# Router head of feed-forward 1 inside the causal attention, and output pieces ahead of query stores

## The reference

```python
x = x + _L0_attn_a_ref(_layernorm(x), Wqkv, Wo)   # 32 heads of 16, one k and v, ALiBi, causal
x = x + _L0_ffn_ref(_layernorm(x), c1_w, c2_w, w1, w2t)
x = x + _L0_attn_b_ref(_layernorm(x), wq, wk, wv, wo)  # 32 heads of 128 on 8, rope, window 128
x = x + _L0_ffn_ref(_layernorm(x), c1_w, c2_w, w1, w2t)
```

```python
inter = xf @ c1_w.T @ c2_w.T
idx = argmax(inter.reshape(n, 56, 32), -1) + arange(0, 1792, 32)
h = relu(einsum('bkm,bm->bk', w1[idx], xf)); out = einsum('bk,bkm->bm', h, w2t[idx])
```

## Time and profile before

| | us |
|---|---|
| median of 3 runs | 2777.52 |
| lowest, highest | 2772.59, 2779.67 |
| profiled execution | 2770.34 |
| its span, first to last instruction | 2768.6 |
| barrier between attention and feed-forward 1, from the span's start | 543.6 to 544.8 |
| PE busy in the span | 2594.3 (94%) |
| DVE, ACT, POOL busy | 1721.9, 1309.1, 1054.8 |
| mean granted clock of PE | 0.964 of 2.4 GHz |

### The profile page before, as it was taken

The page is one execution under the profiler, slowest core; times in us unless marked ns, Lnnn a source line. Parts: engine busy times, 40 slices in busy tenths (PEclk is TensorE's granted clock), DMA queues, the critical chain, the costliest instruction groups (busy, mean ns, idle before and its releaser), DMA issues. The chain is left out here.

```text
span 2768.6 us, 41665 instructions
## 1 busy us (share of the span) xinstructions
PE 2594.3 (94%) x14444; PEld 2026.0 (73%) x14444; DVE 1721.9 (62%) x3488; ACT 1309.1 (47%) x2952; POOL 1054.8 (38%) x938
## 2 busy tenths in 40 slices
PE   4798988889999889999999998999999999799999
PEld 2444443467778678888888876888888888577777
DVE  3674656167777566666566656666666666577775
ACT  2354546332222356566666655566665666232221
POOL 2111122175333344444444423445444443473322
PEclk7899999899999999999999999999999999899999
DMA  5334242220000210111000110111001100300000
GB/s 164 107 94 122 64 117 62 74 84 1 1 0 1 63 31 9 38 38 38 30 18 27 38 39 1 39 39 38 30 8 38 38 23 1 119 1 16 16 15 16
DMA packets 113464, 117.42 MB, mean 42 GB/s; under 512 B 6245, under 2 KB 85989, under 8 KB 113317
## 3 DMA queue, kind: packets, MB, share of 16 engines
q1 hardware_dynamic: 112448, 115.51, 13.7%
q10 hardware_dynamic: 900, 0.40, 0.1%
HBM read 92.09 MB, written 22.68 MB: 41 GB/s over the span
## 5 line engine op out<-in xcount | busy, mean ns | idle before, releaser
L2018 POOL TENSOR_TENSOR rope_straight<-rope_straight,rope_crossed 128x512 f32<-128x512 f32 x160 | 207.0, 1294 | 528.7 <-DVE rope_crossed L1802 528.7
L592 POOL TENSOR_TENSOR f_hidden_low<-f_hidden,f_hidden_high 128x256 fp32r<-128x256 f32 x224 | 183.0, 838 | 400.8 <-ACT f_hidden_high L532 400.6
L1820 DVE TENSOR_TENSOR o_low<-o_sum,o_high 128x512 fp32r<-128x512 f32 x128 | 88.5, 692 | 316.6 <-ACT o_high L1998 316.3
L1029 DVE TENSOR_REDUCE a_max<-a_work 128x1 f32<-128x384 f32 (+3 forms) x352 | 205.3, 635 | 111.8 <-PE a_work L917 110.1
L1912 ACT ACTIVATE probs<-probs,exp_bias 128x256 f32<-128x256 f32 (+1 forms) x512 | 240.3, 471 | 3.3 <-DVE exp_bias L1785 3.2
L1154 ACT ACTIVATE a_probs<-a_scores 128x512 f32<-128x512 f32 x320 | 173.8, 596 | 134.5 <-PE a_scores L931 67.5
L1923 ACT CAST q_high<-rope_straight 128x512 fp32r<-128x512 f32 x128 | 79.5, 621 | 298.6 <-POOL rope_straight L2018 298.6
L1917 ACT ACTIVATE probs<-probs,exp_sum_inverse 128x256 f32<-128x256 f32 (+1 forms) x512 | 205.2, 472 | 32.4 <-DVE exp_sum_inverse L1790 32.4
L532 ACT CAST f_hidden_high<-f_hidden 128x512 fp32r<-128x512 f32 x112 | 69.5, 620 | 309.1 <-PE f_acc L296 170.8
L1622 PE MATMUL w_sum<-o_high,wo_high 128*128 128x512 f32 x512 | 204.9, 400 | 8.7 <-DVE xt L1827 4.8
L1622 PE MATMUL w_sum<-o_high,wo_low 128*128 128x512 f32 x512 | 204.0, 398 | 0.0
(11 more groups left out here) (240 smaller groups left out, 7529.3 us busy)
## 6 DMA issues: line engine op xcount, KB each, us to landing
a_queries<-a_q_stacked SPq DMA_DIRECT2D x16, 1024.0 KB, 6.3
wq_raw<-in_L_attn_b_wq SPq DMA_DIRECT2D x32, 512.0 KB, 3.7
wo_raw<-in_L_attn_b_wo SPq DMA_DIRECT2D x16, 1024.0 KB, 6.4
a_q_stacked<-a_q_part_high SPq DMA_DIRECT2D x32, 256.0 KB
f_w_raw<-in_L_ffn_w SPq DMA_DIRECT2D x14, 512.0 KB, 10.3
f_w_raw<-in_L_ffn_w2t SPq DMA_DIRECT2D x14, 512.0 KB, 11.1
a_q_stacked<-a_q_part_low SPq DMA_DIRECT2D x16, 256.0 KB
wkv_raw<-in_L_attn_b_wk SPq DMA_DIRECT2D x16, 256.0 KB, 6.4
```

Source lines behind the costliest of these rows:

```text
L592: e.tensor_tensor(hl[:, j % 2, cols], hm[:, cols], f32(hh[:, j % 2, cols]), ALU.subtract).then_inc(hl_ready, 1)
L1029: e.tensor_reduce(mx[:, t % 2, to:to + nh], bank, AX.X, ALU.max).then_inc(work_free[k], 1)
L2018: e.tensor_tensor(ra[:, slot], ra[:, slot], rb[:, slot], ALU.add).then_inc(roped, 1)
```

## The change

Four things change; nothing of what is computed does.

1. Feed-forward 1's router T and the masks of its first 256 columns are computed in the attention's last batch: T behind slot 10, the first scores behind slots 12 and 15, with the whole split of c2. c1, c2 and the ranks are loaded at the end of batch 2's query stores, w1's first chunk in the last batch. The tiles lie at addresses that both stages keep. `ffn` skips these steps (`head`); its `BEFORE` holds only the turn of the first mask.
2. SP loads the output pieces right behind the inverses, ahead of query tiles 2 and 3.
3. In batch 0 the query parts use `ath` and `atl` (four tiles each) instead of `qsh` and `qsl` (two).
4. In the prologue the key and value weights are split first and the query weights last, on DVE behind z's low parts; "KV" waits for the first two splits only.

```diff
+        HEAD_AT = {10: ("T", 0), 12: ("I", 0), 15: ("I", 1)}
...
+                    if b == NB - 1 and s in HEAD_AT:
+                        kind, i = HEAD_AT[s]
+                        yield "small", kind, b, i
...
+        def query_parts(b, m):
+            return (ath[:, m], atl[:, m]) if b == 0 else (qsh[:, m % 2], qsl[:, m % 2])
...   PE, small
-                        e.wait_ge(w_low, 3)
+                        e.wait_ge(w_low, 2 if kind == "KV" else 3)
...
+                elif kind == "T":
+                    e.wait_ge(head_in, 16)
+                    e.wait_ge(z_ready, (NB + 1) * DT)
+                    for d in range(DT):
+                        mm = e.matmul(bank[0:CROWS, :], c1s[:, d, :], zf[:, d, :], start=d == 0, stop=d == DT - 1)
+                elif kind == "I":
+                    e.wait_ge(t_low, 1)
+                    e.wait_ge(c2_low, INTER // CH)
+                    for t in (2 * i, 2 * i + 1):
+                        mm = e.matmul(bank[:, t % 2 * CH:(t % 2 + 1) * CH], ts[:, t * P:(t + 1) * P], c2s[:, 0:CH],
+                                      start=True, stop=True)
...   DVE, small
+                elif kind == "T":
+                    e.wait_ge(t_high, 1)
+                    e.tensor_tensor(ts[32:64, :], bank[32:64, :], f32(ts[32:64, :]), ALU.subtract).then_inc(t_low, 1)
...
+                elif kind == "I":
+                    if i == 0:
+                        e.wait_ge(rank_in, 16)
+                        chain(e.tensor_copy(rev[:, :], rank_raw[:, :]))
+                        for k in range(2):
+                            e.wait_ge(q_stored[k], 48 * DT // 2 * NB)
+                        e.wait_ge(c2_low, INTER // CH)
+                    e.wait_ge(full, n)
...   the five steps of find_max, into fmask
...   DVE, plan
                     if step == ["mean", 0, 0]:
-                        low_weights(0, wl[:, :, :], w_raw[:, :, 0:NQ], wh[:, :, :])
-                        low_weights(1, wkvl[:, :, 0:AD], w_raw[:, :, NQ + AD:], wkvh[:, :, 0:AD])
-                        low_weights(2, wkvl[:, :, 32:KV], w_raw[:, :, NQ:NQ + AD], wkvh[:, :, 32:KV])
+                        low_weights(0, wkvl[:, :, 0:AD], w_raw[:, :, NQ + AD:], wkvh[:, :, 0:AD])
+                        low_weights(1, wkvl[:, :, 32:KV], w_raw[:, :, NQ:NQ + AD], wkvh[:, :, 32:KV])
...   at the end of step ["var", 0, 0]
+                        low_weights(2, wl[:, :, :], w_raw[:, :, 0:NQ], wh[:, :, :])
...   ACT
-                    wait(e, q_stored[i % 2], 48 * (DT // 2 * b + i // 2))
-                    e.copy(qsh[:, i % 2], bank[:, :]).then_inc(q_high, 1)
+                    if b:
+                        e.wait_ge(q_stored[i % 2], 48 * (DT // 2 * b + i // 2))
+                    e.copy(query_parts(b, i)[0], bank[:, :]).then_inc(q_high, 1)
+                elif kind == "T":
+                    e.wait_ge(full, n)
+                    e.copy(ts[:, :], bank[0:CROWS, :]).then_inc(t_high, 1)
...
+                    if b == NB - 1 and p < 2:
+                        if p == 0:
+                            e.wait_ge(c2_in, 16)
+                        cols = slice(p * INTER // 2, (p + 1) * INTER // 2)
+                        e.copy(c2s[:, cols], c2_raw[:, cols]).then_inc(c2_high, 1)
...   POOL, ahead of the last batch's out_tile
+                if b == NB - 1:
+                    e.wait_ge(c2_high, 2)
+                    e.wait_ge(zl_ready, (NB + 1) * DT)
+                    for cols in range(0, INTER, CH):
+                        part = c2s[64:CROWS, cols:cols + CH]
+                        e.tensor_tensor(part, c2_raw[64:CROWS, cols:cols + CH], f32(part), ALU.subtract).then_inc(c2_low, 1)
...   SP
                     store_inverses(b - 1)
+                    for m in range(DT):
+                        load_out(b - 1, m)
                 if more:
                     send_queries(b + 1, 2)
                 if b == 0:
                     send_max(0, 2)
-                for m in range(DT) if b else ():
-                    load_out(b - 1, m)
+                if not more:
+                    e.wait_ge(scores_full, (NB - 1) * UNITS_A)
+                    e.dma_start(w1_first[:, :, :], w1[:, 0:2]).then_inc(w1_in, 16)
                 if more:
                     send_queries(b + 1, 3)
                     queries_stored(b + 1)
+                if b + 2 == NB:
+                    e.dma_start(c1s[:, :, :], c1).then_inc(head_in, 16)
+                    e.dma_start(c2_raw[:, :], c2).then_inc(c2_in, 16)
+                    e.dma_start(rank_raw[:, :], rank).then_inc(rank_in, 16)
+                if more:
                     load_queries(b + 1, 0)
                     load_queries(b + 1, 1)
...   ffn
-        BEFORE = [("mean", 0), ("var", 0)] * (not given) + [("T", 0), ("next I", 0), ("next I", 1), ("next M", 0)]
+        BEFORE = [("mean", 0), ("var", 0)] * (not given) + [("T", 0), ("next I", 0), ("next I", 1)] * (not head) + [("next M", 0)]
...
-            router(None)
-            for half in range(2):
-                next_scores(None, half)
+            if not head:
+                router(None)
+                for half in range(2):
+                    next_scores(None, half)
```

128 lines of the change are left out of this document (85 added, 43 removed).

## The result

| | before | after |
|---|---|---|
| median of 6 runs each, us | 2778.44 | 2752.36 |
| lowest, highest | 2772.59, 2781.36 | 2743.99, 2759.56 |
| profiled execution (span) | 2770.34 (2768.6) | 2752.86 (2750.7) |

The ratio is 0.9916, with a 95% interval of 0.9893 to 0.9938: 17 to 30 us faster, 23 by the ratio. The forecast was 2757 and, for the profiled execution, 2749.6. The profiled pair lies 17.9 us apart in span, less than the medians do (26); why is part of what follows.

The account below looks back on a forecast made before the run. PE's waits in the causal attention and at feed-forward 1's start were taken as the bound, stages being separated by barriers. -2.3 - 12.5 + 3.7 - 9.6 = -20.7 us: 2749.6 profiled, 2757 median, range 2747 to 2769.

Parts of the forecast that it names:

- Prologue, minus 2.3: Prologue: splitting key and value weights first brings DVE's variance step 2.3 us sooner; bounds 0 to minus 5.7.
- I take nothing for the buffers: Prologue, batch 0: four query buffers gain 0, as the DMA queue lets nothing flow earlier; bounds 0 and 3.43 us.
- Pieces, minus 12.5: Attention batches 1 and 2: loading output pieces ahead of query stores gains 6.4 and 6.1 us at slot 12.
- Head, plus 3.7: Attention's last batch: T costs 2.95 us, its copy 0.4, c2 copies 0.3; bounds plus 0 and plus 8.4.
- Handover, minus 9.6: Start of feed-forward 1: first up-projection 7.16 us sooner, 2.40 us mask wait gone; bounds minus 6 and minus 12.
- (a): Attention: stores still meet the pieces, slot 12 gains 1.8 us in batch 1, none in batch 2; total -10.0; chance 0.15.
- (b): Last batch: T and the masks cost their upper bound, 8.4 us instead of 3.7; total -16.0, 2761.5; chance 0.15.
- (c): Handover: weights, not router, held PE; if early w1 fails, only the mask's 2.40 us remain; total -13.5; chance 0.06.
- (d): Attention or first up-projections: PE runs a long stretch at 1.2 GHz, for example +19 us, 2797; chance 0.03.
- (e): Buffers (3.4 us) and PE keeping its higher level behind the first mask (2.4) count too: -26.5, 2751; chance 0.11.

Follow-up runs that it names:

- Combined: Changed kernel with c1/c2/rank loads later, tile 3's maxima earlier, w1's first piece split in attention, feed-forward 2's c2 subtraction in six pieces, z announced earlier: 2734.39 us.
- two_buffers: Changed kernel with batch 0's query parts in two buffers again instead of four, new weight order kept: 2754.18 us, ratio to the kernel before 0.9932.
- t_twice: Changed kernel with T's eight matmuls made twice over behind slot 10 of the last batch: 2758.50 us, ratio to the kernel before 0.9944.
- c_late: Changed kernel with c1, c2 and the ranks loaded behind query tile 2's query load in batch 2, not ahead of the query loads: 2751.61 us, ratio 0.9903.
- late_w1: Changed kernel with w1's first piece loaded at feed-forward 1's start again, router and first masks staying in the attention: 2755.01 us, ratio 0.9927.

## Why the prediction was right, step by step

**Prologue, minus 2.3: half right in its reason.** The variance step came 0.15 sooner (18.47 for 18.62), not 2.3. The step that failed is "DVE's variance step then no longer stands behind the split ... and comes 2.3 us sooner": next in line were PE's variance matmuls, and where they run at the 1.2 GHz level they end at 18.4 and take the whole gain. Combined shows the step as foreseen when they don't: 16.28, 2.34 sooner, first scores at 77.57 (forecast 77.4). The second failure is "I take nothing for the buffers": two_buffers has first scores at 81.40, the nine executions with new order and four buffers 77.6 to 80.1, mean 79.1. That is some 2.3 us, from one execution on one side, and it is nearly all of what the prologue gained on the average. I had reasoned from the even DMA share that nothing flows sooner; but ACT and PE waited for those stores, and the next batch's layernorm and maxima with them. All in all 81.6 (mean of four with the old prologue) became 79.1, 2.5 us: the size was right on the average, and in the profiled pair 1.0, as before's had the high level and after's had not.

**Pieces, minus 12.5: right, with a term missing and one too large.** ACT's waits are gone; from first copy to first projection it is 8.35 and 8.36 us (forecast 8.36). The query loads of batch 1 go out at 248.53, 9.0 sooner, 8.0 without the 1.1 that all was sooner by then (query tile 2's first store at 235.18 for 236.26; forecast 8.0). Counted from the first scores, slot 12 comes 7.9 us sooner in batch 1 (forecast 6.4) and 11.7 in batch 2 (forecast 12.5), and 1.8 of it are lost behind that. Batch 1 gained more than 6.4, as the pauses that are gone had stretches at 1.2 GHz behind them. Batch 2 gained less than 6.1: the three loads cost 1.3 on the queue and their bytes another 1.6 (the query loads' issue took 4.25 for 2.69), 2.9 where I had 1.9; the searches of slot 10 then wait 1.99 for queries, which the prediction did not name, and behind the wait at slot 12 (2.38; forecast 2.8) PE falls to the low level. The windows show where each kernel pays. Before:

```profile
252.00:254.00 2.00, 2.00 (x12) 0.50 (x4) 0.58 (x1) 1.13 (x3) 1.29 (x2) 0.50 0.53 200
364.00:366.00 2.00, 2.00 (x12) 0.50 (x4) 1.09 (x2) 0.00 (x0) 0.52 (x1) 0.50 0.55 178
```

After:

```profile
252.00:254.00 2.00, 2.00 (x17) 1.39 (x14) 1.51 (x3) 1.09 (x2) 1.92 (x3) 1.00 1.21 299
384.00:386.00 2.00, 2.00 (x16) 0.37 (x14) 1.25 (x2) 0.99 (x2) 0.00 (x0) 0.50 1.18 325
```

From 155 us behind the first scores, where batch 1 nears its first output projection, to 6 us behind that of batch 2, PE spends 27 to 31 us at the 1.2 GHz level in all five executions with the pieces behind the stores and 10 to 17 in the nine with the pieces ahead (added up from windows of 1 us). Half of the difference of the means, some 8 us of busy time, goes with the order. In the first 155 us that time is 24 us in t_twice and 40 in c_late, whose edits act only in later batches; this is why busy time alone prices little.

Taking the means of five and five executions, the stretch went from 397.3 to 386.1: 11.2, of which 5.2 are idle time and 6.0 busy time. My sum compared start times (11.4 us from first copy to first projection before, 8.36 in batch 3), so it held the slow stretch inside these spans without naming it, and none outside them. That it came close is in part luck: the slow stretches that it left out gave back what the waits that it left out took.

**Head, plus 3.7: right.** T took 3.67 (I had 3.43, of which 0.48 was to hide), ACT stood idle 2.73 behind it and copied for 0.58 (I had 0.4). I0's multiplication took 0.42 with POOL idle. At the same clock of 0.90 the end of the attention is 68.52 before and 71.56 after, plus 3.04: PE is busy 4.25 longer and idle 1.21 less (8.74 to 7.53), where I had let only 0.48 of idle time go. A second T finds nothing more to hide in (t_twice). Over all executions the stretch takes 67.6 in five without the head and 68.6 in eight with it, only 1.0 more, at a mean clock of 0.91 and 0.95; whether the head has a part in the higher clock is not shown.

**Handover, minus 9.6: right.** First up-projection 5.33 behind the start (forecast 5.39), 7.22 sooner (7.16). The wait for the mask is gone, but the stretch got 2.07 and not 2.40 shorter, as the up-projections run at a lower clock (0.71 for 0.82). The two make 9.29, where the sum had 9.6; in means of four and six executions the handover went from 22.6 to 13.0, which is 9.6. The second weight piece came in time.

**The rivals.** (a) is refuted by the query loads (8.0 sooner and not 1.8). (b): the head is not at its upper bound. (c): late_w1 shows that the early load is worth 3.7 of the 7.2; the other 3.5 came from taking router and c2 out of the way, so "the router never held PE" was not tested by itself. (d) did not come. The median of 2752.4 lies nearer to (e), 2751, than to 2757, and one of its grounds, the buffers, is real. The other came true for the clock and not for the time. Behind the first turn of masks PE ran at a low level before and runs at the full one after:

```profile
570.10:573.10 3.00, 3.00 (x8) 2.31 (x7) 2.86 (x6) 0.14 (x1) 1.60 (x2) 0.50 0.00 0
```

```profile
552.94:555.94 3.00, 3.00 (x15) 2.43 (x14) 2.86 (x6) 0.11 (x1) 1.65 (x2) 1.00 0.76 302
...
559.89 0.62 PE L283 MATMUL f_aux<-identb,f_mask 128*128 128x128 bf16 x8 [1.59 <-DVE f_mask L430]
```

But then PE waits 1.59 for the second mask, and the third turn comes 25.73 us behind the first, against 25.79 before.

The 7.2 us that I added between profile and median shrank to nothing for after (2752.86 against 2752.36). Before's profiled execution was 8.1 below its median; 1.8 of that lie in its first 80 us (79.78 against a mean of 81.6), and where the rest lies no trace here shows. By the profiled execution the forecast was 2749.6, and 2752.86 came. By means over the executions of like kernels the parts are minus 2.5, minus 11.2, plus 1.0, minus 9.6 and minus 0.5 for all behind the handover, together minus 22.8, which is the 23 of the ratio. The forecast's minus 20.7 fits that better than the profiled pair's 17.9 does.

Open: why single executions differ at the same place (first scores of one kind of kernel 77.6 to 80.1, end of the attention at 0.90 to 1.00) is not explained by any run here.

## What to carry to other kernels

Put a load whose operands are ready ahead of stores that still wait for theirs: the queue had 11 us in which it stood behind a store that was not ready. Split a stretch's gain into idle and busy time of the bound engine over several executions; a single pair can be off by the clock by as much as a middling term of the sum. Cut a long GpSimd instruction where VectorE works next to it, even if GpSimd itself gets slower by it.

## What the runs showed of the hardware

- One and the same sequence of 2542 matmuls kept PE busy for 343.2 to 354.3 us at mean granted clocks of 0.94 to 0.91; less half of the time spent at the 1.2 GHz level it was 320 to 323 us each time.
- Late output pieces cost PE pauses (2.68 and 2.45 us in batch 1) and, behind these, stretches at the 1.2 GHz level: over batches 1 and 2 the time at that level was 27 to 31 us with the pauses and 10 to 17 without.
- A DVE multiplication of 0.42 us took 3.58 beside one POOL instruction of 3.47 and 0.84 beside six of 0.8 each; the six took 4.80 together.
- A load of 0.88 MB ahead on the queue lengthened the issue of the two loads behind it from 2.5 to 4.25 us, so its price is not only its own issues (1.3).
